# Two pieces of a normalisation pipeline moved to GpSimd in the first dense stage of a graph network layer

## The reference

```python
h = jnp.maximum(_layernorm(x, axis=-1), 0.0)
x = x + _L0_gnn_ref(h, ...)       # (h + neighbours) @ W.T + b, leaky 0.01
h = jnp.maximum(_layernorm(x, axis=-1), 0.0)
x = x + _L1_gnn_ref(h, ...)       # four attention layers, each ending in
                                  # (out - mu) * rsqrt(var + eps) * g + beta
return x
```

## Time and profile before

| | us |
|---|---|
| median of 3 runs | 2285.7 |
| lowest, highest | 2283.72, 2287.53 |
| the profiled execution, its own time | 2294.79 |
| its span, first to last instruction | 2293.1 |

### The profile page before, as it was taken

How to read it: one execution, slowest core, us unless ns; L and a number is a source line. 1 busy time by engine, 2 the same in 40 slices (tenths; PEclk the granted TensorE clock), 3 DMA queues, 4 the chain that set the end, 5 groups by cost and what they waited for, 6 DMA issues and landing times. The chain is left out here.

```text
span 2293.1 us, 41415 instructions
## 1 busy us (share of the span) xinstructions
PE 1745.7 (76%) x9894; PEld 1277.6 (56%) x9894; DVE 1609.0 (70%) x8473; ACT 1513.0 (66%) x7686; POOL 1151.3 (50%) x1069
## 2 busy tenths in 40 slices
PE   2589488888488867866996875996884997884960
PEld 1589355554377764535884544884543885552850
DVE  3671699998599967975555985555995555895860
ACT  0452499999399967963665982665992664993640
POOL 0577777300155538771216772215773224774677
PEclk9995599999599977987996996996995997996985
DMA  7123323221212122212113212113113113123421
GB/s 141 24 51 84 93 78 95 76 64 32 80 51 65 51 64 60 60 46 71 47 47 75 56 42 70 47 47 84 42 46 81 40 45 91 33 51 92 107 70 35
DMA packets 123138, 145.24 MB, mean 63 GB/s; under 512 B 56197, under 2 KB 83637, under 8 KB 122145
## 3 DMA queue, kind: packets, MB, share of 16 engines
q1 hardware_dynamic: 66303, 116.40, 18.6%
q0 software_dynamic: 56160, 25.40, 5.5%
q10 hardware_dynamic: 432, 0.79, 0.1%
HBM read 94.60 MB, written 67.86 MB: 71 GB/s over the span
## 5 line engine op out<-in xcount | busy, mean ns | idle before, releaser
L211 POOL DMA_INDIRECT S<-row_t,rowI x400 | 541.1, 1353 | 232.2 <-issue 232.2
L938 PE MATMUL bank<-AC,XT 128*125 128x390 f32 x800 | 331.6, 521 | 0.4
L1002 ACT ACTIVATE R<-bank 125x128 f32<-125x128 f32 x1200 | 322.8, 305 | 0.0
L1656 POOL TENSOR_TENSOR R<-ident,aselfS 125x250 f32<-125x250 f32 x150 | 90.7, 607 | 391.2 <-PE bank L1684 313.8
L1002 ACT ACTIVATION_READ_ACCUMULATOR R<-bank 125x1 f32 x1200 | 277.1, 239 | 0.0
L1702 PE MATMUL bank<-WCX,XT 128*125 128x130 f32 (+1 forms) x1400 | 250.8, 302 | 0.0
L199 PE MATMUL bank<-ident,Y 125*128 125x125 f32 x800 | 130.8, 289 | 113.4 <-ACT Y L953 58.7
L199 PEld LDWEIGHTS bank<-ident,Y 125*128 125x128 f32 x800 | 98.1, 150 | 213.7 <-issue 139.0
L1789 DVE COPY XT<-bank 128x250 f32<-128x250 f32 x150 | 62.8, 418 | 210.4 <-PE bank L199 210.4
L1702 PEld LDWEIGHTS bank<-WCX,XT 128*125 128x125 f32 x1400 | 182.7, 189 | 43.4 <-issue 1.6
L1044 DVE BATCH_NORM_STATS2 st<-R 125x6 f32<-125x128 f32 x800 | 173.7, 282 | 30.5 <-issue 30.1
(11 more groups left out here) (418 smaller groups left out, 5173.1 us busy)
## 6 DMA issues: line engine op xcount, KB each, us to landing
row_t<-T SPq DMA_DIRECT2D x40, 568.8 KB
R<-in_x SPq DMA_DIRECT2D x100, 224.0 KB
out_rows<-R SPq DMA_DIRECT2D x100, 224.0 KB
R<-m_t SPq DMA_DIRECT2D x5, 2734.4 KB
S<-row_t,rowI POOLq DMA_INDIRECT x400
T<-in_edge_attr SPq DMA_DIRECT2D x1, 5600.0 KB
x_t<-XB SPq DMA_DIRECT2D x50, 112.0 KB
R<-x_t SPq DMA_DIRECT2D x25, 224.0 KB
```

Source lines behind the costliest of these rows:

```text
L211: pool.indirect_dma_start(to, None, table, bass.IndirectOffsetOnAxis(ap=idx, axis=0), bounds_check=rows - 1, oob_is_err=False).then_inc(do ...
L938: nc.tensor.matmul(LAYERS[a][0:P, 0:3 * D + 6], h0(g, a), ACB[:, 0:3 * D + 6], start=True, stop=True).then_inc(layers_done.s, 1)
L1002: ins = nc.scalar.activation(JUNK[:, a * 3 + l, :], LAYERS[a][0:P, l * D:(l + 1) * D], ACT.Square, scale=D ** -0.5, accum_out=NRM[:, g % N ...
```

## The change

`dense` gets a flag `pool_rows`, set in the first call only. With it, GpSimd runs `normalise2` for rows 0 and 1 of group t - 2 and then `add_beta` for group t - 3 at the head of each slot, ahead of the slot's gathers; ScalarE's list loses `normalise2` and VectorE's loses `add_beta`. The four later calls are as before.

```diff
-        def dense(first_group, groups, moves, move, arrive):
+        def dense(first_group, groups, moves, move, arrive, pool_rows=False):
...
                 @block.gpsimd
                 def _(pool):
+                    def normalise2(g):
+                        pool.wait_ge(*scaled2.at(g + 1))
+                        if g >= 2:
+                            pool.wait_ge(*turned2.at(g - 1))
+                        for a in range(2):
+                            ins = nc.gpsimd.tensor_scalar(Y[:, 2 + g % 2, a, :], rows(g)[:, a, :], rr2[:, g % NS, a:a + 1],
+                                                          nm2[:, g % NS, a:a + 1], ALU.mult, ALU.add)
+                        ins.then_inc(y2_scalar.s, 1)
+
+                    def add_beta(g):
+                        pool.wait_ge(*turned2.at(g + 1))
+                        nc.gpsimd.tensor_tensor(rows(g), rows(g), B3[:, :].unsqueeze(1).broadcast_to([P, Q, D]),
+                                                ALU.add).then_inc(beta_added.s, 1)
+
                     done = 0
                     for t in slots:
+                        if pool_rows:
+                            run(t, [(2, normalise2), (3, add_beta)])
                         upto = moves * min(t + 1, groups) // groups
                         move(pool, done, upto)
...
+                    if pool_rows:
+                        ops = [o for o in ops if o[1] is not normalise2]
...
+                    if pool_rows:
+                        ops = [o for o in ops if o[1] is not add_beta]
...
-        dense(0, SHARES[0], TC, first_moves, [(s_xsrc, 16 * C), (s_xdst, 16 * TC)])
+        dense(0, SHARES[0], TC, first_moves, [(s_xsrc, 16 * C), (s_xdst, 16 * TC)], pool_rows=True)
```

More of the change, by code:

```diff
@@ L1030, in root_last @@
                         nc.scalar.activation(rt4[:, g % NS, :], chain(g)[:, 8, :], ACT.Sqrt).then_inc(last_root.s, 1)
-                    for t in slots:
[L1033 to L1037, removed]
+                    ops = [(3, copy2), (6, square_last), (0, root1), (1, copy1), (2, root2),
+                           (5, s_root(2, third_sum, s3_ready)), (6, root_last),
+                           (4, s_root(0, first_sum, s1_ready)), (3, norms(0)), (3, norms(1)), (2, normalise2),
+                           (5, copy_s), (4, s_root(1, second_sum, s2_ready)), (1, slope), (0, normalise1),
+                           (3, norms(2)), (3, norms(3))]
+                    if pool_rows:
+                        ops = [o for o in ops if o[1] is not normalise2]
+                    for t in slots:
+                        run(t, ops)
                 @block.vector
@@ L1200, in finish @@
                         nc.vector.tensor_tensor(rows(g), rows(g), FR[:, g % 2, :, :], ALU.add).then_inc(out_ready.s, 1)
-                    for t in slots:
[L1203 to L1207, removed]
+                    ops = [(3, normalise2), (0, statistics1), (2, leak), (5, with_s2), (2, join),
+                           (0, aggregate1), (2, statistics2), (5, times_s2), (2, aggregate2), (4, sums),
+                           (5, third), (6, sum_last), (7, multiply), (0, invert1), (6, invert_last),
+                           (2, invert2), (0, scale1), (5, fourth), (4, with_s1), (2, scale2), (4, times_s1),
+                           (0, normalise1), (4, second), (7, finish), (6, add_beta)]
+                    if pool_rows:
+                        ops = [o for o in ops if o[1] is not add_beta]
+                    for t in slots:
+                        run(t, ops)
             for sig in (counted1, var1, rooted1, inverted1, scaled1, y1_vector, y1_scalar, turned1, copied1, conv_done,
```

## The result

The changed kernel takes 2302.24 us (median) beside 2287.26 for the kernel before in the same comparison. The ratio is 1.0079 with a 95% interval of 1.0054 to 1.0104: 18 us slower, 12 to 24. Forecast were 19 us slower. The profiled execution took 2303.71 us.

What follows compares the result with a forecast made beforehand. VectorE was taken as the bound at 8.53 us per front slot. Per slot -0.60 + 1.25 = +0.65 us, over 29 slots +18.9, took the median from 2285.7 to 2304.6 us; whole range 2266 to 2322.

Steps and rivals of the forecast that it cites:

- What bounds the kernel: In the front's steady slots VectorE is a true bound at 8.53 us per slot; ScalarE, as full, may be one too.
- The saving of 0.60 us: VectorE loses the 125x512 addition of line 1194 in each front slot: 8.53 - 0.60 = 7.93 us.
- The holds, 1.25 us (1.02 to 1.41): Per front slot, VectorE waits at the shared SBUF port for GpSimd's two tensor_scalar (0.17 each at most) and add_beta (0.85 to 1.07).
- GpSimd's prices: Per slot on GpSimd: 0.30 us for each of two tensor_scalar, 1.2 for add_beta, together 1.8; 7.2 with gathers.
- The signs: Expected profile: front slots near 9.2 us, later calls 8.53, one VectorE operation about 1 us longer, ScalarE gaps, GpSimd awaiting scale2.
- 29 slots: From first to last steady front slot, a per-slot change counts 29 times: +0.65 us gives +18.9 us.
- No cost from the new waits: Waits of GpSimd's normalise2, add_beta and gathers, and TensorE's turn2, cost zero; gathers end near 540 us, turn2 has 1.8 us cover.
- No hold that matters: Rival: GpSimd's work slides under VectorE's one-input or PSUM operations, front slots run at 7.93 us, time 2268; chance 0.24.
- GpSimd as the bound: Rival: GpSimd's three moved operations cost 4 us, making its front slot 9.4 us with gathers, time 2312; chance 0.04.
- The rule of the Trainium skill: VectorE instructions with two SBUF inputs or in two-port mode and GpSimd instructions reading SBUF exclude each other for a whole instruction.

Runs made afterwards that it cites:

- the best kernel: Against the changed kernel, add_beta runs ahead of normalise2 on GpSimd, with a memset and a wait clearing the gathers before it; ratio to before 0.9939, again 0.9958.
- the one-input operation: Against the changed kernel, GpSimd's beta addition became a tensor_scalar with two constants over the same 125x512 rows, beta left out; ratio to before 0.9983.
- the timed one: Against the kernel with memset and wait behind the gathers, add_beta also waits for VectorE's sum_last, the step ahead of multiply; ratio to before 1.0000.

## Why the prediction was right, point by point

- **What bounds the kernel.** VectorE at 8.53 us per slot. Right, by `normalise2` moved alone: relieving ScalarE by 0.77 us gave no gain. ScalarE needs 8.40.
- **The saving of 0.60 us.** Right to the hundredth: 8.10 in the best kernel is 8.53 - 0.60 + 0.16.
- **The holds, 1.25 us (1.02 to 1.41).** Measured 1.26, but made up otherwise. `add_beta` held `finish` for 1.10, forecast 1.07 less what line 1093 might absorb; it met neither line 1093 nor line 1150, which the prediction had named. The two `tensor_scalar` of GpSimd cost 0.16 together where I had 0.17 each, and the second of line 1142 was not held at all. That the total fell between the bounds is the mechanism's merit. That it met the 1.25 to a hundredth is luck: 1.25 was picked between the bounds, and an `add_beta` at the upper end and a pair at half its price cancelled.
- **GpSimd's prices.** `add_beta` 1.26, forecast 1.2. The `tensor_scalar` are recorded with 0.47 each, forecast 0.30 (0.28 to 0.60). But this is not their own price: GpSimd waits for VectorE too. Near the end of the front of the changed kernel line 1112 has no more work, and `finish` starts at the same time as GpSimd's second `tensor_scalar`; VectorE, then GpSimd:

```profile
570.79 0.69 DVE L1219 TENSOR_TENSOR R<-R 125x512 f32<-125x512 f32 x1
571.41 1.64 DVE L1121 TENSOR_SCALAR Y<-R,rr,nm 125x128 f32<-125x128 f32 x2
...
570.77 0.95 POOL L874 TENSOR_SCALAR Y<-R,rr,nm 125x128 f32<-125x128 f32 x1
571.69 1.27 POOL L880 TENSOR_TENSOR R<-R,B 125x512 f32<-125x512 f32 x1
```

  Here `finish` takes its usual 0.69, and GpSimd's operation 0.95: it ends 0.24 us after `finish`. With `normalise2` moved alone, where `finish` and `add_beta` of VectorE both come at that place, it takes 1.47. So its own work is about 0.25 us or less (an estimate from these rows), near the forecast, and a part of each 0.47 is a wait for VectorE. This also tells, as a reading, why the pair costs VectorE only 0.16 where the one-input operation on 512 elements holds for 0.44. The last two rows show once more that VectorE's `tensor_scalar` pair is held to the end of `add_beta`: 1.64 instead of 0.59.
- **The signs.** All came: slots of 9.18 us and 8.53 in the later calls, one VectorE operation (line 1200 of before) longer by 1.1 us and ending with GpSimd's addition, ScalarE idle for 1.07 us per slot (28.57 of 246), GpSimd idle until `scale2`.
- **29 slots.** 29 x 0.65 = 18.9; `scale2` of the last group comes at 577.72 instead of 558.73, 19.0 us later.
- **No cost from the new waits.** Right for the gathers and for GpSimd's half. The last gather starts at 568.17, not near 540 as forecast, and this cost nothing either: behind the front nothing got longer. The step did not look at TensorE, which now stands idle for 1.12 us in most slots, in one piece, behind VectorE's late half (and for 0.25 elsewhere), where in the slot of the earlier trace rows it had two pauses of 0.64 and 0.50. Its clock, 1.00 all through the steady slots before, now falls to 0.50 of full (1.2 GHz) eight times in the steady slots. Rows of one stretch at the upper level and of one fall of each kind:

```profile
320.00:327.00 7.00, 5.62 (x29) 3.27 (x28) 7.00 (x36) 6.27 (x39) 4.38 (x6) 1.00 0.17 50
327.50:330.50 3.00, 3.00 (x9) 1.84 (x8) 3.00 (x26) 2.94 (x18) 1.68 (x2) 0.50 0.45 125
365.00:371.50 6.50, 6.50 (x18) 3.91 (x17) 6.50 (x37) 4.96 (x28) 4.17 (x5) 0.50 0.14 42
```

  Five of the eight are short, like the one at 327.5, and the slots around them took 9.17 to 9.19 us: they cost nothing. Three are twice as long (at 365, 457 and 549), and the slot that follows took 9.51 or 9.52 instead of 9.18: 1 us in all. In other kernels of this study falls cost more, 8 us in the timed one (four slots of 10.4 to 10.5 where 8.36 is usual). That the new pause brings the falls is not shown, and the last section speaks against it.
- **The rivals.** "No hold that matters" is out as a description of this kernel, and its number, 2268, is near what becomes of it once the addition lies elsewhere (14 and 10 us under before in two comparisons, against the 17 of the rival). GpSimd as the bound is out: it waits 2.13 us per slot.
- **The rule of the Trainium skill** ("SBUF — State Buffer", section "Who interferes with whom"), which the prediction weighed: the runs agree for a GpSimd operation with two inputs and with one, and for `tensor_scalar` on VectorE (0.41 us of hold). GpSimd's two short `tensor_scalar`, 0.94 us long in sum, hold VectorE for only 0.16; as they wait for VectorE themselves, this does not contradict "fully blocks". The rows also show that the recorded starts do not tell who waits: at 570.77 GpSimd's operation is recorded 0.02 us ahead of `finish` and is the one that waits, while at 406.31 `add_beta` is 0.04 us ahead and is the one that goes on.

## What to carry to other kernels

Work moved from a full VectorE to an idle GpSimd is not priced by its own length but by what VectorE has in hand while it runs: the same addition cost 0, 1.10 or 1.81 us per slot. Look in VectorE's timeline for a run of operations with one input, or from PSUM, as long as the GpSimd operation, and tie the start to it; where a gather stands ahead in GpSimd's queue, put a tiny operation and a wait for its end between. Then see what sets the pace next: with `add_beta` alone moved it was ScalarE at 8.40 us, with both moved TensorE's clock in single slots.

## What the runs showed of the hardware that was not expected

- A GpSimd operation that stands directly behind a gather in the queue holds VectorE already during the gather: 1.81 us for an operation of 1.27, the hold beginning 0.71 us ahead of the operation's recorded start. With a memset and a wait between, the hold there was zero. That the operation had begun on part of GpSimd is my reading; shown is that the memset with its wait removes it.
- The hold goes both ways. A GpSimd `tensor_scalar` of 125x128 is recorded with 0.45 us beside tiny steps of VectorE and with 0.95 beside a 125x512 addition, and the addition is not slowed. So a recorded duration on GpSimd can be half a wait, and is no price.
- TensorE's granted clock stayed at 1.00 through the steady slots of the kernel before and of the one that moves `add_beta` alone. In every kernel with `normalise2` on GpSimd it fell to 0.50 between three and nine times from 297 to 543 us, but for one run: two runs of one and the same kernel (the gathers cleared) had 0.97 and 1.00 over the front. The length of a single pause does not sort them: the kernel before pauses for up to 0.85 us in one piece and keeps the clock, and in the one with the one-input operation it falls seven times though no pause is longer than 0.56 us. What decides it is open.
